# Two adapted linear layers for 32 sequences: a start in finer steps, identity matmuls as spare work, and LoRA-B matmuls set apart

## The reference

```python
# layer 0: LoRA adapter of each sequence, id from 1 to 7, rank 16
base  = einsum('bsi,oi->bso', x, weight) + bias
low   = einsum('bsi,bri->bsr', x, lora_a[adapter_id])
delta = einsum('bsr,bor->bso', low, lora_b[adapter_id])
x = x + base + scale[adapter_id][:, None, None] * delta
# layer 1: each sequence has one of 14 full 2048 x 2048 matrices
x = x + einsum('bij,bkj->bik', x, weight1[adapter_ids])
```

## Time and profile before

| | us |
|---|---|
| median of 3 runs | 2699.63 (2698.18 to 2702.82) |
| the profiled execution | 2697.91 |
| its span in the trace | 2696.1 |
| TensorE busy | 2684.3 (12826 matmul instructions) |
| VectorE, ScalarE, GpSimd busy | 1782.7, 1329.9, 730.5 |

### The profile page before, as it was taken

The page is one execution under the profiler, slowest core; times in us unless marked ns, Lnnn a source line. Parts: engine busy times, 40 slices in busy tenths (PEclk is TensorE's granted clock), DMA queues, the critical chain, the costliest instruction groups (busy, mean ns, idle before and its releaser), DMA issues.

```text
span 2696.1 us, 35567 instructions
## 1 busy us (share of the span) xinstructions
PE 2684.3 (100%) x12826; PEld 2225.0 (83%) x12826; DVE 1782.7 (66%) x1582; ACT 1329.9 (49%) x1398; POOL 730.5 (27%) x586
## 2 busy tenths in 40 slices
PE   8999999999999999999999999999999999999999
PEld 7888888888888888888888888888888888888887
DVE  7758776867455557686745555678674565667865
ACT  3423366666432426666633233566663323456665
POOL 6345611413412111150342111124034111112402
PEclk9999999999999999999999999999999999999999
DMA  8868865677645536668764454889986445489886
GB/s 296 307 233 326 290 203 203 234 272 252 223 152 172 171 110 209 210 233 273 254 207 151 169 179 145 306 309 330 371 333 209 152 157 198 139 304 314 312 322 231
DMA packets 192784, 637.91 MB, mean 237 GB/s; under 512 B 22464, under 2 KB 30816, under 8 KB 192608
## 3 DMA queue, kind: packets, MB, share of 16 engines
q1 hardware_dynamic: 185408, 609.94, 65.6%
q10 hardware_dynamic: 7200, 25.69, 2.4%
HBM read 643.93 MB, written 58.72 MB: 261 GB/s over the span
## 4 chain that ended last, share of the span: by engine, by line
PE 98%; POOL 0%; DMA 0%; DVE 0%; SPq 0%; issue 0%; ACT 0%; POOLq 0%; ACTq 0%
PE acc L971 17%; PE acc L972 17%; PE acc L973 17%; PE acc L918 15%; PE acc L919 15%; PE acc L928 15%; PE acc L874 1%; PE acc L940 1%; POOL raw L584 0%; PE acc L926 0%; DMA raw<-xt 0%; DVE ws L835 0%; DVE ops L835 0%; DMA cb<-xt 0%; DMA cb<-ids 0%
## 5 line engine op out<-in xcount | busy, mean ns | idle before, releaser
L835 DVE TENSOR_TENSOR ws<-raw,ws 128x1024 fp32r<-128x1024 f32 x1020 | 1327.7, 1326 | 432.2 <-ACT ws L710 427.6
L710 ACT CAST ws<-raw 128x1024 fp32r<-128x1024 f32 (+1 forms) x1052 | 1078.5, 1051 | 1047.7 <-PE acc L973 475.9
L971 PE MATMUL acc<-ws,ops 128*128 128x512 f32 (+1 forms) x2048 | 796.9, 389 | 0.0
L972 PE MATMUL acc<-ws,ops 128*128 128x512 f32 (+1 forms) x2048 | 796.9, 389 | 0.0
L973 PE MATMUL acc<-ws,ops 128*128 128x512 f32 (+1 forms) x2048 | 796.8, 389 | 0.0
L918 PE MATMUL acc<-ops,ws 128*128 128x512 f32 x1776 | 693.8, 391 | 0.2
L919 PE MATMUL acc<-ops,ws 128*128 128x512 f32 x1776 | 692.2, 390 | 0.0
L928 PE MATMUL acc<-ops,ws 128*128 128x512 f32 x1776 | 691.4, 389 | 0.0
L616 POOL TENSOR_TENSOR raw<-raw,eye_s 128x128 f32<-128x128 f32 x384 | 350.6, 942 | 1176.8 <-DMA raw<-w 1176.4
L973 PEld LDWEIGHTS acc<-ws,ops 128*128 128x128 f32 x2048 | 384.4, 188 | 80.0
L971 PEld LDWEIGHTS acc<-ws,ops 128*128 128x128 f32 x2048 | 384.4, 188 | 79.5
(11 more groups left out here) (64 smaller groups left out, 583.5 us busy)
## 6 DMA issues: line engine op xcount, KB each, us to landing
raw<-w SPq DMA_DIRECT2D x920, 512.0 KB
raw<-w_sums SPq DMA_DIRECT2D x104, 512.0 KB
raw<-xt SPq DMA_DIRECT2D x96, 512.0 KB
out<-ost SPq DMA_DIRECT2D x128, 256.0 KB, 6.8
cb<-xt SPq DMA_DIRECT2D x60, 512.0 KB, 5.9
w_sums<-raw ACTq DMA_DIRECT2D x32, 512.0 KB, 6.6
ost<-a SPq DMA_DIRECT2D x64, 128.0 KB, 3.0
x_sums<-raw ACTq DMA_DIRECT2D x16, 512.0 KB, 4.3
```

The costliest lines, as they stand in the source:

```text
L710: ins = eng.copy(hi, src)
L835: ins = eng.tensor_tensor(lo, src, hi, ALU.subtract)
L971: eng.matmul(acc, yh, wh, start=begin, stop=False)
L972: eng.matmul(acc, yh, wl, start=False, stop=False)
```

## The change

- At the start SyncE requests the first halves of sequences 0 and 2, ScalarE those of 1 and 3 (before: 0 and 1, 2 and 3). ScalarE reads the number of one sequence before each request instead of both first.
- The second weight tile gets the key -40.5, so it is split behind the first two half blocks of x.
- The 12 spare matmuls of 512 columns on the first weight tile go. In their place 3 matmuls on `eye_s` (128x128, plain f32) stand behind the counting, with a wait for `eye_s`, and 11 behind the sorting.
- W(0,0,0) and W(0,0,1) are done for each part of the rows and for two sequences at a time, so with 96 matmuls of 256 columns instead of 48 of 512. Tile 1 takes its low weight part last.
- The two LoRA-B matmuls are parted. In product 3, q = 0 stands at t = 5 of the tile and q = 1 at t = 7. In the others, q = 0 of LB stands at t = 5 of the W block ahead of it, with its waits, and q = 1 stays where LB was. Where an LB follows an S block, both stay.

```diff
-WARM = 12
+WARM = (3, 11)
+LB_AT = 5
...
-        splits.append(((-100.0, -38.5)[n] if n < 2 else key, ts[at[b]], b[0], b[1:]))
+        splits.append(((-100.0, -40.5)[n] if n < 2 else key, ts[at[b]], b[0], b[1:]))
...
-                    for b in range(2):
-                        batches.append(load_order(eng, 0, 0, b, b + 1)[0])
-                        load_first(eng, 0, b, batches[b])
-                    registers[0, 0] = batches + list(load_order(eng, 0, 0, 2, 4))
+                    for b in (0, 2):
+                        batches += load_order(eng, 0, 0, b, b + 2 if b else 1)
+                        load_first(eng, 0, b, batches[b // 2])
+                    registers[0, 0] = [batches[0], load_order(eng, 0, 0, 1, 2)[0]] + batches[1:]
...
-            batches = load_order(eng, 0, 0, 2, 4)
-            for b in range(2):
-                load_first(eng, 0, 2 + b, batches[b])
+            for b in (1, 3):
+                load_first(eng, 0, b, load_order(eng, 0, 0, b, b + 1)[0])
...
+            def lora_b(acc, i, o, q, stop):
+                cols = slice(2 * P * q, 2 * P * q + 2 * P)
+                return eng.matmul(acc[:, cols], bs[0:96, i % 2, q, P * o:P * o + P], lows[0:96, cols],
+                                  start=False, stop=stop, skip_group_check=stop)
+
+            def lora_b_first(b):
+                _, g, k, o = b
+                i = LORA_K.index(k)
+                if o == 0:
+                    eng.wait_ge(s_lo, max(number["BS", g, i, q] for q in range(2)) + 1)
+                    eng.wait_ge(s_low, 4 * g + 2 * (i // 2) + 2)
+                if k == 6:
+                    eng.wait_ge(s_ev0, ev_no[g, 6, o, 0])
+                lora_b(bank_of(b)[:], i, o, 0, True)
+
+            def warm(n):
+                for _ in range(n):
+                    eng.matmul(bank[0][:, 0:P], eye_s[:], eye_s[:], start=True, stop=True)
...
+            eng.wait_ge(s_eye, 16)
+            warm(WARM[0])
             eng.wait_ge(s_key, 9)
...
-            eng.wait_ge(s_hi, 1)
-            for i in range(WARM):
-                eng.matmul(bank[0][:], ws[:, 0, 0, 0:P], ws[:, 0, 0, 0:512], start=True, stop=True)
+            warm(WARM[1])
...
+                        for part, two, o2 in itertools.product(range(2), repeat=3):
+                            early = o2 and not part and not two
+                            if early:
+                                eng.wait_ge(s_hi, number["W", 0, 0, 1] + 1)
+                            cols = slice(2 * P * two, 2 * P * two + 2 * P)
+                            n, acc = slot_of["W", 0, 0, o2], bank_of(("W", 0, 0, o2))[:, cols]
+                            for w, v in ((0, 0), (0, 1), (1, 0)) if o2 else ((0, 0), (1, 0), (0, 1)):
+                                if w == o2 == 0:
+                                    eng.wait_ge(s_lo if v else s_hi, number["XH", part, 2 * two + 1] + 1)
+                                elif w and early:
                                     eng.wait_ge(s_lo, number["W", 0, 0, 1] + 1)
...
-                        if t == HT - 1 and k == 3:
+                        if t in (LB_AT, HT - 1) and k == 3:
                             i = LORA_K.index(k)
-                            if o == 0:
+                            if o == 0 and t == LB_AT:
                                 eng.wait_ge(s_lo, max(number["BS", g, i, q] for q in range(2)) + 1)
...
+                            lora_b(acc, i, o, int(t == HT - 1), False)
+                        if t == LB_AT and after_it[0] == "LB":
+                            lora_b_first(after_it)
                         ins = eng.matmul(acc, wl, xh, start=False, stop=(t == HT - 1))
...
+                    if before[0] != "W":
+                        lora_b_first(blk)
+                    lora_b(bank_of(blk)[:], LORA_K.index(k), o, 1, True).then_inc(s_mm, 1)
```

More of the change, by code:

```diff
@@ L1 @@
+import itertools
 from contextlib import ExitStack
@@ L851, in _ @@
             eng.matmul(bank[6][:, 0:NB], wide, put, start=True, stop=True).then_inc(s_put, 1)
-            eng.wait_ge(s_hi, 1)
-            for i in range(WARM):
-                eng.matmul(bank[0][:], ws[:, 0, 0, 0:P], ws[:, 0, 0, 0:512], start=True, stop=True)
-            for blk in blocks:
+            warm(WARM[1])
+            for before, blk, after_it in zip([("begin",)] + blocks, blocks, blocks[1:] + [("end",)]):
                 if blk == ("W", 0, 0, 2):
@@ L884, in _ @@
                     if g == k == o == 0:
-                        for part in range(2):
-                            for o2 in range(2):
-                                if o2 and not part:
-                                    eng.wait_ge(s_lo, number["W", 0, 0, 1] + 1)
[L889 to L897, removed]
+                        for part, two, o2 in itertools.product(range(2), repeat=3):
[8 more added lines that the diff above has]
+                                elif w and early:
+                                    eng.wait_ge(s_lo, number["W", 0, 0, 1] + 1)
+                                for t in range(4 * part, 4 * part + 4):
+                                    ins = eng.matmul(acc, ws[:, n, w, P * t:P * t + P], ops[:, t, v, cols],
+                                                     start=(two == w == v == t == 0), stop=((v, w)[o2] == 1 and t == HT - 1),
+                                                     skip_group_check=True)
+                            if part and two:
+                                ins.then_inc(s_mm, 1)
                         continue
@@ L931, in _ @@
                     _, g, k, o = blk
[L932 to L938, removed]
-                        cols = slice(2 * P * q, 2 * P * q + 2 * P)
-                        ins = eng.matmul(acc[:, cols], bs[0:96, i % 2, q, P * o:P * o + P], lows[0:96, cols],
-                                         start=False, stop=True, skip_group_check=True)
-                    ins.then_inc(s_mm, 1)
+                    if before[0] != "W":
+                        lora_b_first(blk)
+                    lora_b(bank_of(blk)[:], LORA_K.index(k), o, 1, True).then_inc(s_mm, 1)
                 else:
```

## The result

| | us |
|---|---|
| before, median of 18 runs | 2699.63 (2697.93 to 2705.73) |
| after, median of 18 runs | 2703.39 (2701.9 to 2709.69) |
| ratio, 95% interval | 1.0018 (1.0011 to 1.0024) |
| the profiled execution after | 2705.49, span 2703.7 |

The account below looks back on a forecast made before the run. TensorE's instructions plus its few waits were taken to bound the kernel. The profiled 2697.91 us plus 0.0 for the start and 0.0 for LoRA-B gave 2697.9; the median's 1.7 above that made 2699.6 us, range 2694.8 to 2704.2.

Parts of the forecast that it names:

- rival 2: LoRA-B: a whole tail behind each parted short matmul, +3.3 us, 2702.9 us; chance 0.12.
- rival 3: Start: its chain of waits moves by one turn of GpSimd, giving 2697.2 to 2702.0 us; chance 0.08.
- I take half, 13 ns for each: LoRA-B: each parted short matmul leaves half a pair's tail, so parting costs 0.0 us.
- The 0.92 us in the prediction: After LoRA-A: four matmuls take 0.92 us instead of 0.907, read as half a tail or more from one disturbance.
- Inside the pair no tail is seen between its two: LoRA-B: no tail between a pair's two matmuls, taken as speaking for less tail behind a single one.
- the block of x at 21.7 us shouldn't either: Start: the product 1 block of x that GpSimd begins on should not move from its 21.7 us landing.
- All of the early start is given back: Start: TensorE arrives early at W(0,0,5) but waits 2.8 us there, until 42.3 us; net 0.0 us.
- rival 4: Start: TensorE's clock falls in the new 2.8 us wait and must rise again, 2702.4 us; chance 0.05.
- the first stage's 0.12 us for each 256-wide matmul: First two tiles: 96 matmuls of 256 columns at 0.12 us each, 11.5 us against 11.0 before.
- the spare matmuls: Start: 6 instructions end at 5.2 us without delaying the order; 22 more take 5.2 us, ending at 11.4.
- the covered waits of product 6: LoRA-B: the first matmul meets VectorE's partial sum 1.6 us earlier, still covered by 0.7 us for LB(6,0).
- rivals 5 and 6: LoRA-B: uncovered weight loads, 2708.4 us, chance 0.05; or no tails and more load overlap, 2694.2 us, chance 0.03.

Follow-up runs that it names:

- e1_lora: The kernel before with only the LoRA-B matmuls parted as in the change: 2701.27 us, ratio 1.0012.
- e5_patterns: The kernel before with one 512-column matmul per block cut into pieces in layer 1, side by side or apart: halves parted by six cost 53 ns, by one 73.
- e9_late: The kernel before, but SyncE waits for batch 3's half block instead of batch 0's ahead of its next transfers: 2701.95 us, ratio 1.0011.
- e2_start: The changed kernel with the LoRA-B matmuls as pairs again, so the start's changes alone: 2701.04 us, ratio 1.0011.
- e11_start_free: The changed start with LoRA-B in pairs, without SyncE's wait for batch 0 and with TensorE's flags read early: 2702.47 us, ratio 1.001.
- e15_start_held: e11_start_free with 30 spare matmuls instead of 11 ahead of the first tiles, to hold TensorE back: 2700.94 us, ratio 1.0009.
- e16_again: The same kernel as e11_start_free, run for a second profile: that execution took 2700.25 us at full clock.
- e10_free: The kernel before without SyncE's wait for batch 0's half block ahead of its next transfers: 2698.16 us, ratio 0.9998.
- e4_start_oldqueues: The changed start with LoRA-B in pairs, but the queues of the kernel before: 2700.33 us, ratio 1.0011.
- e6_quads: The kernel before with the LoRA-B pairs of two tiles side by side, four short matmuls in a row: 2698.24 us, ratio 0.9995.
- e14_quads_free: The kernel before with LoRA-B in fours, except product 5 of the first group, and without SyncE's wait for batch 0: 2698.65 us, ratio 0.9998.

## Why the prediction failed, step by step

The forecast was no change, 2699.6 us. It came out at 2703.39: inside the range of 2694.8 to 2704.2, and less than 0.2% off, but slower and clear of its interval where I had expected the same time. What costs it is a sum of two things, one near rival 2 and one that no rival held. (Two ends in the text are off by its own terms: 2702.9 and 1.5 make 2704.4 as the upper end of the range, and in rival 3 0.2 and 0.3 us gained would give 2699.1 and not 2697.2.)

**The tail of a single LoRA-B matmul** is the step that failed most. "I take half, 13 ns for each" was mis-sized. It is the whole tail, 26 ns, for each: 120 more runs of short matmuls x 26 = 3.1 us in place of 0.0. Rival 2 gave 3.3, e1_lora measured 3.1. The rows that I had for it said so. Behind LoRA-A, the matmuls of the earlier trace rows start 236, 228, 232 and 231 ns apart, the last four steps of the tail, 20 of its 26 ns. The 0.92 us in the prediction is the difference of two rounded starts. Unrounded it is 0.927, so that 20 ns became 13, and 13 was my half. I weighed it against "Inside the pair no tail is seen between its two", which is no evidence, since there the change from short to long is still to come. e5_patterns shows this directly.

**"the block of x at 21.7 us shouldn't either"** was wrong: it moved by 2.06 us. One part of it is seen. With two halves requested at 6.77 and 6.84 us, batch 0's landed at 10.32 instead of 9.60 us, and between 9.85 and 10.3 us in the other profiles with the new queues. SyncE waits for just that one, and its queue went on 0.7 us later. I had cost the exchange for who comes first, and not for the wait on SyncE's queue that hangs on one of them. e9_late prices such a delay: 3.3 us late costs 3.2 to 4.0. The other part isn't SyncE's wait. GpSimd began at 22.64 us with it (e2_start) and at 22.6 to 22.8 without it (e11_start_free, e15_start_held, e16_again). The queues alone gave 22.06, the finer start alone 21.71. What makes the block late when both are there isn't shown.

**"All of the early start is given back"** held at the tile I named: W(0,0,5) started at 42.34 us, 42.4 forecast, though the wait moved to W(0,0,4). The split for W(0,0,4), taken as done at 32.5 us, ended at 36.69. What I left out is that the relay goes on behind it. In product 1 each tile goes from GpSimd to VectorE (the sum), ScalarE, VectorE, TensorE and back to SyncE's next request. W(0,1,7), whose tile was split 0.4 us before it was needed, is the last gate. Its split ended at 100.72 us before and at 101.07 when TensorE was ahead by 1.2 us (e10_free). A gain is cut off at such tiles and a delay of the relay is passed on. With the start of before, SyncE's wait in it or not, it ended at 100.7 to 101.5 us, once at 102.3; with the changed one at 101.2 to 101.5 in three profiles and at 101.8 to 103.5 in four. So the changed start comes later on the whole, and part of what one pair of profiles shows is scatter. Of the 1.4 to 2.9 us that the start costs in the medians, this is what can be pointed at.

**The wait for the flags** was not in the sum. The eight values need 3.2 us of TensorE's sequencer, and it began on them at 21.07 us, two microseconds ahead of the last of the 96 starts at 23.09. With matmuls of 512 columns it had been some 4 us ahead. Changing the width of the matmuls halves the time for which the queue covers the sequencer. It cost 1.2 us at W(0,0,2) (24.39 for 23.2 forecast), which the next wait swallowed.

**The clock** (rival 4) may have acted, though not at W(0,0,5). In the changed kernel three of 18 runs had a mean clock of 0.999, and took 2707.4 to 2709.7; the median of the others is 2703.12. But a mean below 1 isn't always a loss: in e4_start_oldqueues eight of 10 runs had one, the fastest (2698.46) among them. e6_quads shows one fall in a profile, behind 2.2 us of waiting. The Trainium skill (TensorE: Matmul & The Clock Gate, section Why this matters for your kernels) warns of idle gaps between bursts of matmuls. The trace agrees in kind, with 3.41 us at half clock, which cost 1.7, though behind a shorter gap than the page speaks of. In which wait the unprofiled runs fell, if they did, is not shown; W(0,5,7) is where the only profiled one did.

**What held:** the first stage's 0.12 us for each 256-wide matmul (0.122 measured, no tail inside a run of short ones), its start (11.63 for 11.4), the spare matmuls (22 instructions in 5.1 us, no delay of the order), the covered waits of product 6, rivals 5 and 6 not seen.

**Open:** why the changed start, held back and with SyncE's wait removed, still loses 2.3 us (in its profile 1.0 us is the overshoot), and why W(0,5,7), 250 us later, waits 0.5 to 2.2 us in several kernels, one of them with the first tiles and the queues of before (e14_quads_free), and not at all in a second profile of the changed kernel. My guess is that both hang on how transfers, GpSimd and VectorE fall into step in the first group. No run here separates them.

## What to carry to other kernels

Keep short matmuls together: the price is in the return from short to long, once for each run of short ones. Before such a price is read from two rounded starts, read every step between them. Before transfers change queues, look for what waits on the landing of the first. And where TensorE is 100% busy, an earlier start is worth only the smallest margin of all tiles behind it. Read these margins down the whole relay, not at the first tile that waits.

## What the runs showed of the hardware that I had not expected

- After a run of 256-wide matmuls, five of 512 columns start 233, 236, 228, 232 and 231 ns apart instead of 227, 26 ns in all, to within a ns or two a step whether the run was one, two or four long. A piece of 128 columns costs more: 384 and 128 in place of 512 took 87 ns more, four of 128 took 233.
- Two short matmuls one or three matmuls apart cost more than two six apart (73 and 67 against 53 ns, tails in full).
- In one profile (e6_quads) TensorE's clock fell to 1.2 GHz 0.6 us after a wait of 2.2 us in the midst of dense work, for 3.41 us. Behind waits of 1.53 us (the changed kernel) and 1.55 (e11_start_free) it stayed at 2.4.
- 96 matmuls of 256 columns in a row, with a weight load of 188 to 192 ns recorded for each, ran at 0.12 us each.
